# A row-by-row recurrence on one core: sweeps as three batch chains in column tiles of 32, PE's sweep a hardware loop, two state slots

## What is computed

```python
def _sweep(x, w, b, axis, reverse):
    rows = jnp.moveaxis(x, axis, 0)
    if reverse:
        rows = rows[::-1]
    def step(prev, row):
        new = row + jax.nn.relu(_conv1d(prev, w, b))   # 32 -> 32 channels, 9 taps
        return (new, new)
    _, rest = jax.lax.scan(step, rows[0], rows[1:])
    ...
out = _sweep(x, w_d, b_d, axis=2, reverse=False)
out = _sweep(out, w_u, b_u, axis=2, reverse=True)
out = _sweep(out, w_r, b_r, axis=3, reverse=False)
out = _sweep(out, w_l, b_l, axis=3, reverse=True)
```

## Time and profile before

| | us |
|---|---|
| median of 3 runs | 636.95 |
| lowest, highest | 630.97, 639.58 |
| the profiled execution | 637.02 |
| its span, first to last instruction | 635.2 |
| the four sweeps within it (L1108 first to last) | about 291 to 532 |

### The profile page before, as it was taken

One profiled execution on the slowest core, in us unless ns is written; L12 is line 12 of the kernel. 1 busy time (PEld: TensorE's weight loads), 2 busy tenths in 40 slices (PEclk: granted clock), 3 DMA queues, 4 the chain that ended last, 5 costly groups with the idle time before them and its releaser, 6 DMA issues.

```text
span 635.2 us, 22695 instructions
## 1 busy us (share of the span) xinstructions
PE 573.7 (90%) x9860; PEld 524.2 (83%) x9860; DVE 360.1 (57%) x823; ACT 318.7 (50%) x842; POOL 99.2 (16%) x220
## 2 busy tenths in 40 slices
PE   8978798999997999988999999489999999486897
PEld 7978797999996977978999888489999999386773
DVE  3747989656459836463454545245554543398326
ACT  4756988552277302444444444234447776268400
POOL 4000000000021000001333333423330144220000
PEclk9989989999998989998999999879999999886769
DMA  9730773060000000000000033310000444200006
GB/s 353 307 133 1 267 279 124 1 265 1 2 1 2 2 19 1 0 1 2 4 5 4 4 86 81 92 19 5 4 4 12 78 75 71 43 0 1 2 3 264
DMA packets 54442, 41.53 MB, mean 65 GB/s; under 512 B 49350, under 2 KB 49478, under 8 KB 53126
## 3 DMA queue, kind: packets, MB, share of 16 engines
q1 hardware_dynamic: 53816, 39.29, 19.4%
q0 software_dynamic: 384, 0.39, 0.3%
q10 hardware_dynamic: 144, 0.39, 0.2%
HBM read 27.49 MB, written 4.19 MB: 50 GB/s over the span
## 4 chain that ended last, share of the span: by engine, by line
PE 68%; DVE 18%; SPq 5%; ACT 5%; issue 2%; DMA 1%; POOL 0%; DVEq 0%; ACTq 0%
PE PS L718 35%; PE PS L434 6%; DVE RB L955 5%; PE PS L687 5%; PE PS L637 3%; SPq L317 3%; DVE sums L994 3%; SPq L328 2%; DVE RCD L1006 2%; PE PS L584 2%; PE PS L533 2%; PE PS L540 2%; PE PS L509 2%; PE PS L554 2%; DVE RCD L1029 1%
## 5 line engine op out<-in xcount | busy, mean ns | idle before, releaser
L718 PE MATMUL PS<-RE,conv_sb 128*64 128x64 f32 x6048 | 231.7, 231 | 10.1 <-DVE RE L1096 8.6
L718 PEld LDWEIGHTS PS<-RE,conv_sb 128*64 128x64 f32 x6048 | 212.0, 139 | 29.8 <-DVE RE L1096 9.3
L848 ACT COPY PS<-convb_sb 128x64 f32<-128x64 f32 x504 | 108.1, 215 | 119.2 <-DVE RE L1108 106.2
L1108 DVE SCALAR_TENSOR_TENSOR RE<-PS,RCD 128x64 f32<-128x64 f32 x252 | 56.5, 224 | 58.2 <-PE PS L718 50.0
L392 POOL COPY RCD<-RE 128x128 f32<-128x128 f32 x126 | 37.0, 294 | 175.0 <-DVE RE L1108 175.0
L1108 DVE SCALAR_TENSOR_TENSOR RE<-PS,RE 128x64 f32<-128x64 f32 x126 | 32.5, 259 | 29.8 <-PE PS L718 25.6
L781 ACT COPY RB<-PS 32x256 f32<-32x256 f32 x64 | 41.7, 652 | 7.8 <-PE PS L493 7.0
L955 DVE COPY RB<-PS 32x256 f32<-32x256 f32 x64 | 41.6, 649 | 6.2 <-PE PS L493 5.4
L1108 DVE SCALAR_TENSOR_TENSOR RE<-PS,RB 128x64 f32<-128x64 f32 x126 | 28.2, 224 | 28.2 <-PE PS L718 28.2
L455 PE MATMUL PS<-warm 128*128 128x128 bf16 x468 | 36.4, 248 | 6.3 <-ACT RCD L821 3.6
L455 PEld LDWEIGHTS PS<-warm 128*128 128x128 bf16 x468 | 33.6, 113 | 7.3 <-ACT RCD L821 3.9
(11 more groups left out here) (117 smaller groups left out, 778.4 us busy)
## 6 DMA issues: line engine op xcount, KB each, us to landing
RE<-wspec SPq DMA_DIRECT2D x8, 2048.0 KB, 8.7
RA<-x_in SPq DMA_DIRECT2D x8, 512.0 KB, 7.6
RCD<-x_in SPq DMA_DIRECT2D x1, 4096.0 KB, 13.4
out<-RA SPq DMA_DIRECT2D x8, 512.0 KB, 2.7
RCD<-RB SPq DMA_DIRECT2D x48, 64.0 KB, 2.6
RE<-RCD SPq DMA_DIRECT2D x32, 80.0 KB, 2.6
RE<-RCD SPq DMA_DIRECT2D x16, 64.0 KB, 2.1
RCD<-RB SPq DMA_DIRECT2D x26, 32.0 KB, 1.9
```

The source lines that it names most:

```text
L718: m = pe.matmul(conv_bank(s, u, c)[o:o + OC], conv_sb[:, s, d, o:o + OC], prev, start=False, stop=(d == 2), skip_group_check=True)
L848: act.copy(banks_of, convb_sb[:, s:s + 1].unsqueeze(2).to_broadcast([P, c1 - c0, n])).then_inc(s_seed, 1)
L1108: dve.scalar_tensor_tensor(out=state[:, state_slot(s, u), b0:b1, 1:1 + HO], in0=conv_bank(s, u, c), scalar=0.0, in1=row_at(SRC[s], s, q, u ...
```

## The change

CHAINS becomes three chains of 3, 3 and 2 images (48, 48 and 32 columns) and OC becomes 32, so that a tap has four column tiles. A row then has 3 x 3 x 4 matmuls, 72 passes. SEEDS seeds chains 0 and 1 with one instruction and chain 2 with another; six banks are used instead of four. On PE the rows 2 to 63 of a sweep are a hardware loop of 31 turns (Fori) with two rows in a turn, row 1 ahead of it; the values of the waits within depend on the loop's counter, which is a register. Which slot and bank a row uses depends on its parity alone. There are two state slots instead of four, and DVE waits for the copy of row r - 2 ahead of row r. DVE's, ACT's and POOL's programs stay unrolled.

```diff
--- before.py
+++ after.py
@@ -20,9 +20,9 @@
 NW = 4
 WRUN = W // NW
 MO = P // 2
-CHAINS = ((0, 4), (4, 8))
-OC = P // 2
-SEEDS = ((0, 1), (1, 2))
+CHAINS = ((0, 3), (3, 6), (6, 8))
+OC = P // 4
+SEEDS = ((0, 2), (2, 3))
 KYC = 4
 NCH = KY // KYC
 X8 = H // 2 // Q
@@ -154,8 +154,8 @@
         X3 = RA[:, :].rearrange("p (k t i w o) -> p k t i w o", k=NW, t=BH, i=Q, w=WRUN)
 
 
-        state = RE[:, 2 * WCOLS + 3072:2 * WCOLS + 3072 + 4 * B * (HO + 2)].rearrange(
-            "p (s b v) -> p s b v", s=4, b=B)
+        state = RE[:, 2 * WCOLS + 3072:2 * WCOLS + 3072 + 2 * B * (HO + 2)].rearrange(
+            "p (s b v) -> p s b v", s=2, b=B)
 
         def by_run(ap, k):
 
@@ -269,7 +269,7 @@
 
         def state_slot(s, u):
 
-            return (u + 3 * (s % 2)) % 4
+            return (u + s) % 2
 
         def conv_bank(s, u, c):
 
@@ -707,20 +707,22 @@
                 m = pe.matmul(PS[:, bank, 0:P], warm[:, :], warm[:, :], start=True, stop=True)
             m.then_inc(s_bits, 1)
             for s in range(4):
-                def step(q, u):
+                def step(r, odd=1):
                     for c, (b0, b1) in enumerate(CHAINS):
-                        pe.wait_ge(s_st, state_count(s, Q * q + u - 1, c))
+                        pe.wait_ge(s_st, state_count(s, r - 1, c))
                         if c == SEEDS[seed_of(c)][0]:
-                            pe.wait_ge(s_seed, len(SEEDS) * (63 * s + Q * q + u - 1) + seed_of(c) + 1)
+                            pe.wait_ge(s_seed, len(SEEDS) * (63 * s + r - 1) + seed_of(c) + 1)
                         for d in range(3):
-                            prev = state[:, state_slot(s, u - 1), b0:b1, d:d + HO]
+                            prev = state[:, (s + odd - 1) % 2, b0:b1, d:d + HO]
                             for o in range(0, P, OC):
-                                m = pe.matmul(conv_bank(s, u, c)[o:o + OC], conv_sb[:, s, d, o:o + OC], prev,
+                                m = pe.matmul(conv_bank(s, odd, c)[o:o + OC], conv_sb[:, s, d, o:o + OC], prev,
                                               start=False, stop=(d == 2), skip_group_check=True)
                         m.then_inc(s_cv, 1)
 
-                for r in range(1, H):
-                    step(r // Q, r % Q)
+                step(1)
+                with pe.Fori(1, H // 2) as pair:
+                    step(2 * pair, 0)
+                    step(2 * pair + 1, 1)
 
             experts(1)
 
@@ -1101,10 +1103,10 @@
                     for c, (b0, b1) in enumerate(CHAINS):
                         r = Q * q + u
                         dve.wait_ge(s_cv, len(CHAINS) * (63 * s + r - 1) + c + 1)
-                        if c == 0 and s == 3 and r > Q:
-                            dve.wait_ge(s_arl, r - Q)
-                        elif c == 0 and 63 * s + r > Q:
-                            dve.wait_ge(s_arc, 63 * s + r - Q)
+                        if c == 0 and s == 3 and r > 2:
+                            dve.wait_ge(s_arl, r - 2)
+                        elif c == 0 and 63 * s + r > 2:
+                            dve.wait_ge(s_arc, 63 * s + r - 2)
                         dve.scalar_tensor_tensor(out=state[:, state_slot(s, u), b0:b1, 1:1 + HO], in0=conv_bank(s, u, c),
                                                  scalar=0.0, in1=row_at(SRC[s], s, q, u)[:, b0:b1, :],
                                                  op0=ALU.max, op1=ALU.add).then_inc(s_st, 1)
```

## The result

| | us |
|---|---|
| before, median of 4 runs (lowest, highest) | 635.23 (630.97, 639.58) |
| after, median of 4 runs (lowest, highest) | 689.96 (684.72, 696.40) |
| ratio, 95% interval | 1.083 (1.069 to 1.098): slower |
| the profiled execution of after, its span | 684.72, 682.9 |

A forecast was written before the change was run, and what follows sets the result against it. Before, one chain's loop set the 0.90 us row; after, PE's sequencer would: 0.43 + 0.20 + 0.42 + 0.08 = 1.13 us, +0.23 x 252 = +58 us on 637, forecast 695 us, range 608 to 790.

The forecast's parts named there:

- What bounds the kernel before: In the sweeps, one chain's loop (matmuls, DVE, next row's matmuls) sets the row: parts sum to 0.89 us, period 0.90.
- Rival 3: On the array, four tiles don't run side by side or starts have a floor: 2.1 us a row, 940 us; chance 0.08.
- its form from the Trainium skill: On the array, a floor of about 25 ns between small matmuls: 1.8 us a row, kernel at 865 us.
- The sequencer's sum: PE's sequencer work per row in the loop: 1.13 us against 0.90 before, so +0.23 us x 252 rows, +58 us.
- (a): PE's plain matmul and load instructions, 144 a row at 3 ns each: 0.43 us a row (0.29 to 1.1).
- (b): PE's waits not carried by a load: two seed waits a row, 0.20 us; five would be 0.5.
- (c): PE's register operations making the wait values: 7 a row at 60 ns, 0.42 us; bounds 3 ns and 0.1 us each.
- (d): PE's loop branch once in two rows, with the counter's addition: 0.08 us a row.
- Hardly differing between the third and the others: Sign in the next profile: sweeps of some 71 us each, DVE's extra 30 ns in the third no longer in the path.
- The rest of the kernel is not touched, so the whole forecast is the time of a row: Outside the four sweeps nothing changes, so the forecast counts only the time of a row, times 252 rows.
- Rival 1: PE's sequencer keeps up, register operations below some 20 ns: 610 us, at most 618; chance 0.28.
- Rival 4: The loop's back edge fetches code again: one late block a turn adds 0.58 us a row, 840 us; two, 990; chance 0.06.

The follow-up runs named there:

- experiment 7: Changed kernel with PE's register work removed (a semaphore per chain, DVE waits for seeds) and six rows a turn instead of two: 668.8 us, ratio 1.047.
- the seed experiments: Changed kernel with three seed groups instead of two: 700.6 us, ratio 1.110; with one seed group for all three chains: 684.7 us, ratio 1.075.
- experiment 6: Changed kernel with six rows in a turn of PE's loop instead of two, register work kept: 694.8 us, ratio 1.086.
- experiment 5: Changed kernel with PE's register work removed (a semaphore per chain, loop counter as wait value, DVE waits for seeds), two rows a turn: 654.2 us, ratio 1.027.
- experiment 1: Changed kernel with PE's sweep unrolled again; three chains, column tiles of 32 and two slots stay: 931.2 us, ratio 1.480.
- experiment 8: Changed kernel with PE's register work removed (a semaphore per chain, DVE waits for seeds) and four rows a turn instead of two: 666.2 us, ratio 1.049.

## Why the prediction held

*What bounds the kernel before* held. The row of before is the loop of one chain; finer chains without a sequencer in the way shorten it, from 0.90 to 0.83 us (experiment 7's fastest turns), where the prediction had 0.79. The parts of a chain's loop are as said: in the second sweep of after 0.257 us to issue a chain of 48 columns, 0.267 to DVE's start, 0.209 of DVE, and 0.055 to the next matmul where nothing holds PE (experiment 7): 0.79.

*Array, chains, DVE.* Groups of four tiles start every 42.7 ns in the 48-column chains and every 32 in the other (45 and 34 said); DVE's operation takes 208 and 192 ns (205, 187), in the third sweep 231 and 203. Rival 3 is refuted with that: four tiles do run side by side. So is its form from the Trainium skill (TensorE: Matmul & The Clock Gate, Back-to-back issue gap): four starts in 43 ns, passage after passage, are 11 ns each and not 25.

*The sequencer's sum* came out at 1.09 us a row for a typical turn against 1.13 said (1.15 as the mean over all rows), and the sweeps grew by 60 us against 58. That agreement is better than its terms are:

| term, us a row | said | measured |
|---|---|---|
| (a) plain instructions | 0.43 (3 ns each) | 0.29 (2.0 ns) |
| (b) waits of their own | 0.20 | 0, they ride on register operations and loads |
| (c) register operations | 0.42 (7 x 0.06) | 0.56 (5.5 x 0.10) |
| (d) branch and counter | 0.08 | 0.13, the counter's operation counted in (c) |
| held by the array | 0 | 0.11 |

The mis-sized terms are (c), whose upper bound of 0.1 us was the true value, and (b), for which I had not thought of a register operation as something that can carry a wait. They cancel, and that is luck: the mechanism was right and the sum's closeness is not evidence for its terms. What the sum lacked is the last line: the sequencer's work sets a row only where the array has nothing queued. That made my prices for the seed experiments (25 us for an operation) and for tiles of 64 too high by a factor of two and more.

*The signs.* "Hardly differing between the third and the others" held (72.0 beside 69.4 and 72.6; before, the third stood out by 4 us); that DVE's longer operation no longer matters is what a sequencer-bound row should show. The pauses stand in front of chains, the blocks fell by 42 (45 said). Not foreseen: a first sweep of 76.4 us, and rows that alternate between 0.9 and 1.3, since I had spread the branch over both.

*"The rest of the kernel is not touched, so the whole forecast is the time of a row"* failed by 13 us in the profiled execution. The stretch between the second and the third sweep became 3.7 us shorter, and the end 11. For the first, transfers that the longer sweeps cover are a likely cause, not a shown one. For the end they are not: it does not go with the length of the sweeps (experiment 6, with sweeps as long as after's, has 104.0 us, experiment 5, with shorter ones, 93.2) but with the granted clock there. The five profiles with 0.87 to 0.89 have an end of 92 to 94 us, the nine with 0.76 to 0.82 one of 100 to 109. What makes the clock go one way or the other no run separates; runs of one kernel go with it too: after's four have 684.7 and 685.4 us at a mean clock of 0.96, and 694.5 and 696.4 at 0.94. The profiled execution of before had 0.944 and that of after 0.96, so +47.7 flatters the change; the median gives +55.

*Rival 1* (the sequencer keeps up) hung on a register operation under 20 ns; it is 100. The first register operation measured would have decided the case. *Rival 4* is refuted for the loop as it is, since no block comes in its turns, and was underrated in what it says about code: I wrote that unrolled the new form would need a block every 1.4 us and did not ask whether one can come that often. One can come every 3.7, and this number governs experiment 1 and the first passes in experiments 6, 7 and 8.

*Where the loss lies.* The sweeps took 230 us before and 290 after. The finer chains without loop work would have gained (0.90 - 0.83) x 252 = 17 us. The branch, 124 x 0.27 = 33, turns that into +16. Experiment 5's sweeps are 26 longer than before's: some 6 of the missing 10 are its first sweep's slower turns (30 x 0.19), and up to 7 DVE's waits for ACT's copy in the fourth. (Its median is only 14 above before's, with an end that is 10 us shorter.) The register work adds the last 34. No form with the loop or the finer chains that was run is faster than the kernel before: what the finer chains can win is smaller than what either way of bringing them their instructions cost, streamed or looped. Three chains with tiles of 64, unrolled, were not run; at 14.5 ns an instruction their 72 a row would come in 1.04 us, an estimate, still above the 0.90 of before.

## What to carry over

Before making a stream of small matmuls a loop, count two things per turn: the instructions that only the sequencer executes, at 0.1 us each on PE and 0.27 for the branch, and where the array's queue is empty when they come; those are paid, the others hide for the most part. Let the loop's counter be the wait value itself, with one semaphore for each producer, and the register work goes. And before making a stream of matmuls finer, divide its instructions by its time: PE's code came at no more than 252 instructions in 3.7 us, unrolled as well as in the first pass of a loop's body.

## What the runs showed of the hardware that I had not expected

- PE's code comes at one block of 252 instructions every 3.7 us when it is the bound, though the block's transfer takes 0.96 us.
- A register operation of PE's sequencer is shown with 32 to 68 ns and takes about 100 from start to start. It can carry a wait; one that did, with 48 plain instructions behind it, took 194 ns, a wait of its own with the same behind it 207.
- A compare-and-branch is shown with 208 ns (76 to 235) and takes 266. The Trainium skill (Advanced Engine Details and Errata, Control Flow Timing) has 108 for one; the runs here have twice that.
- A loop body of 900 PE instructions is not fetched again in its later turns.
- The same loop body took 2.39 us a turn in one place of the code and 2.18 to 2.27 in others. With a block boundary placed in its first matmuls, the stretch there took 194 and 356 ns by turns.
- Waiting that the profile gives to a seed of ACT was the sequencer's. The seed named there had ended 0.8 us or more before; the operations on the sequencer's own rows were what filled the gap.
